# Differential attention on one core: the weighing of the last work tile ahead of the turning of the present one

## The reference, cut to what matters

```python
def _diff_attn(x, Wq, Wk, Wv, lq1, lq2, lk1, lk2, Wo, bo):
    q = (x @ Wq.T).reshape(b, n, H, D, 2).transpose(0, 1, 4, 2, 3).reshape(b, n, 2 * H, D) * scale
    k = (x @ Wk.T).reshape(b, n, H, D, 2).transpose(0, 1, 4, 2, 3).reshape(b, n, 2 * H, D)
    v = (x @ Wv.T).reshape(b, n, H, 2 * D).transpose(0, 2, 1, 3)
    att = softmax(nan_to_num(einsum('bnqd,bnkd->bnqk', q, k)))
    att6 = att.reshape(b, n, 2, H, 2, H)
    att2 = att6[:, :, 0, :, 0, :] - lam * att6[:, :, 1, :, 1, :]
    out = einsum('bnah,bhnd->bnad', att2, v)
    out = _rmsnorm(out) * (1.0 - LAMBDA_INIT)
    return out.reshape(b, n, d) @ Wo.T + bo
```

## Time and profile before

| what | us |
|---|---|
| median of 3 executions | 3107.2 (3105.85 to 3109.8) |
| the profiled execution, its own time | 3109.19 |
| its span in the profile | 3107.4 |
| differential attention, from the first scores to the last weighing | 2635.6 to 2728.3 |

### The profile page before, as it was taken

The page is one execution under the profiler, slowest core; times in us unless marked ns, Lnnn a source line. Parts: engine busy times, 40 slices in busy tenths (PEclk is TensorE's granted clock), DMA queues, the critical chain, the costliest instruction groups (busy, mean ns, idle before and its releaser), DMA issues. The chain is left out here.

```text
span 3107.4 us, 55478 instructions
## 1 busy us (share of the span) xinstructions
PE 2913.5 (94%) x23641; PEld 2312.9 (74%) x23644; DVE 1612.5 (52%) x3377; ACT 1191.8 (38%) x1885; POOL 84.0 (3%) x67
## 2 busy tenths in 40 slices
PE   6998997999989999999999999999999978689987
PEld 3444776788877888888888888888888867567864
DVE  4333523544454555555554555555555464764487
ACT  2212222333233444344433444334443331635675
POOL 0000101000000000000000000000000013010000
PEclk9999998999999999999999999999999989689988
DMA  7987010111211111101110111101111017705300
GB/s 262 319 288 255 1 44 25 41 41 61 81 51 49 46 47 33 32 28 47 46 33 25 36 47 46 33 23 38 46 41 41 29 45 149 77 31 166 115 15 28
DMA packets 174040, 222.36 MB, mean 72 GB/s; under 512 B 56416, under 2 KB 109664, under 8 KB 173424
## 3 DMA queue, kind: packets, MB, share of 16 engines
q1 hardware_dynamic: 146064, 198.01, 21.1%
q10 hardware_dynamic: 27744, 20.98, 3.0%
HBM read 206.36 MB, written 10.49 MB: 70 GB/s over the span
## 5 line engine op out<-in xcount | busy, mean ns | idle before, releaser
L91 PE MATMUL xa_J<-xa_c_hi,xa_wk_hi 128*128 128x402 f32 x1024 | 364.5, 356 | 4.3 <-ACT xa_kT L1944 3.0
L2056 DVE CUSTOM_DVE_ANT_0 xa_pr<-xa_S,xa_m 128x402 f32<-128x402 f32 x512 | 271.0, 572 | 166.0 <-PE xa_S L2205 166.0
L92 PE MATMUL xa_J<-xa_c_lo,xa_wk_hi 128*128 128x402 f32 x1024 | 354.1, 346 | 0.0
L93 PE MATMUL xa_J<-xa_c_hi,xa_wk_lo 128*128 128x402 f32 x1024 | 354.1, 346 | 0.0
L91 PE MATMUL xa_J<-xa_wv_hi,xa_c_hi 128*128 128x512 f32 (+1 forms) x832 | 335.3, 403 | 0.0
L93 PE MATMUL xa_J<-xa_wv_hi,xa_c_lo 128*128 128x512 f32 (+1 forms) x832 | 327.3, 393 | 0.0
L92 PE MATMUL xa_J<-xa_wv_lo,xa_c_hi 128*128 128x512 f32 (+1 forms) x832 | 327.3, 393 | 0.0
L1944 ACT ACTIVATE xa_kT<-xa_J,cl_bk 128x402 f32<-128x402 f32 x256 | 151.7, 593 | 457.5 <-PE xa_J L93 457.5
L2083 DVE TENSOR_TENSOR cl_v<-xa_J,cl_bv 128x512 f32<-128x512 f32 (+1 forms) x208 | 143.5, 690 | 262.0 <-PE xa_J L93 224.3
L1960 ACT ACTIVATE xa_pr<-xa_pr,xa_nm 128x1608 f32<-128x1608 f32 x128 | 208.6, 1632 | 95.0 <-DVE xa_nm L2072 95.0
L91 PEld LDWEIGHTS xa_J<-xa_c_hi,xa_wk_hi 128*128 128x128 f32 x1024 | 192.7, 188 | 66.3 <-ACT xa_kT L1944 42.9
(11 more groups left out here) (461 smaller groups left out, 5499.1 us busy)
## 6 DMA issues: line engine op xcount, KB each, us to landing
bl_rows<-in_ctx SPq DMA_DIRECT2D x40, 1024.0 KB, 8.3
main_x<-in_ctx_cols SPq DMA_DIRECT2D x192, 201.0 KB, 3.0
bl_cols<-in_ctx_cols SPq DMA_DIRECT2D x24, 1024.0 KB, 10.4
main_qoT<-in_L_ffn_w ACTq DMA_DIRECT2D x32, 512.0 KB, 3.8
main_x<-in_ctx_cols SPq DMA_DIRECT2D x64, 197.5 KB, 2.7
moe_raw<-in_L_ffn_routed_w SPq DMA_DIRECT2D x24, 512.0 KB, 4.1
main_qoT<-in_L_attn_W SPq DMA_DIRECT2D x16, 512.0 KB, 3.7
bl_early<-in_ctx SPq DMA_DIRECT2D x8, 768.0 KB, 12.6
```

Of the source, the lines that this page charges most:

```text
L91: pe.matmul(out, w_hi, x_hi, start=first, stop=False)
L92: pe.matmul(out, w_hi, x_lo, start=False, stop=False)
L93: return pe.matmul(out, w_lo, x_hi, start=False, stop=last)
L2056: nc.vector.tensor_tensor_reduce(out=pr[:, r, ks], in0=S[:, r, 0:KG], in1=m[:, ks], scale=1.0, scalar=NEVER, op0=ALU.add, op1=ALU.max, acc ...
```

## The change

In TensorE's loop over the work tiles the call of `weigh(w - 1)` moves from the end of the round to a place ahead of `turn(w)`. Nothing else changes.

```diff
                 for w in range(WORK):
                     if w + 2 < WORK:
                         scores(w + 2)
+                    if w:
+                        weigh(w - 1)
                     turn(w)
                     if w >= 2:
                         if w - 2 == QUARTERS:
                             pe.wait_ge(ms_ready, 1)
                         mean_squares(w - 2)
-                    if w:
-                        weigh(w - 1)
                 turn_spread(0)
```

## The result

| kernel | median us | runs | ratio to the kernel before, 95% interval |
|---|---|---|---|
| before | 3108.5 | 6 | 1 |
| changed | 3119.5 | 6 | 1.0034 [1.0023, 1.0045] |

0.34% of 3108.5 is 10.6 us, between 7.1 and 14.0. The forecast was +5.8 us (3113.0), in a range to 3121. So the sign and the range held and the size was too small: 3119.5 lies above the forecast's own band (3110 to 3117) and in the band of rival C (3119 to 3123). The profiled execution of the changed kernel took 3116.28 us, the fastest of its six, against 3109.19 for the one of before.

What follows compares the result with a forecast made beforehand. No engine fills the stretch; waits set it, and after the change a serial TensorE-ScalarE loop. Turn(1) +1.7, turn(2) +3.0, five rounds +4.3, tail -3.2 give +5.8 us: 3113.0 us, range for 8 in 10 3103 to 3121.

Steps and rivals of the forecast that it cites:

- the forecast's own band: Whole kernel: the likeliest case, +2.5 to +10 us, its own range 3110 to 3117 us; chance 0.6.
- rival C: Rounds all at half clock, 10.9 us, and one more stand: +12 to +16 us, 3119 to 3123; chance 0.12.
- The serial loop: TensorE with ScalarE, per tile: turn, widen, keep, weigh, next turn, nothing overlapping; 10.0 us a round.
- turn(1), later than before by: TensorE: turn(1) starts at 2661.0 behind weigh(0), against 2659.28 before; +1.7 us.
- turn(2), later than before by: TensorE: turn(2) starts at 2675.9 behind weigh(1), against 2671.22 before; +3.0 us more, to 4.7.
- five rounds, turn(2) to turn(7): TensorE's loop: five rounds of 10.0 us for the 45.7 there were; +4.3 us.
- tail, turn(7) to the end of weigh(7): End of the stage: 8.1 us where it was 11.33, as weigh(6) moved ahead of turn(7); -3.2 us.
- The expected gain: VectorE's three stops for scores: weigh leaves TensorE's path, 5.6 us instead of 9.2; up to 9.64 us back.
- The stand in weigh(1): TensorE waits for program at weigh(1)'s 73rd multiplication, 3.8 us, moving turn(2) from 2672.0 to 2675.9.
- rival A: No wait for program in weigh(1): turn(2) at 2672.0, +1.9 us, 3109; chance 0.18.
- Rival B: Loop at full clock price of 8.4 us, no stand, VectorE the bound: 6.2 us earlier, 3101; chance 0.1.

Runs made afterwards that it cites:

- e1: Changed kernel with keep(w-1) ahead of widen_all(w) on ScalarE; 3111.6 us, ratio 1.0009 to the kernel before.
- e7: The changed kernel run again, nothing edited; 3118.9 us, ratio 1.0034 to the kernel before.
- e2: Changed kernel with extra identity transposes, result unused, ahead of weighings 1 to 6; 3114.5 us, ratio 1.0022 to the kernel before.
- e12: Changed kernel with 20 small unused products (40 multiplications in the trace) ahead of turn(0); 3119.0 us, ratio 1.0034 to the kernel before.
- e9: Changed kernel with keep ahead of the four copies and unused identity transposes ahead of the weighings; 3109.6 us, ratio 1.0000 to the kernel before.
- e4: Kernel before with ScalarE's exp(w+1) moved behind widen_all(w); 3122.8 us, ratio 1.0047 to the kernel before.
- e3: Changed kernel with ScalarE's exp(w+1) moved between widen_all(w) and keep(w-1); 3125.3 us, ratio 1.0051 to the kernel before.

## Why the prediction was right in kind and low in size

**The serial loop** was right: turn, copies, keep, weigh, next turn, every turning after turn(0) and every weighing of tiles 1 to 6 was released as forecast. e1 takes one link out and gives its size back.

**Its price was the term that was mis-sized.** The prediction put "1.64 + 5.24 + 3.03 + 0.1 = 10.0 us a round", and by a second way 1.09 and 3.6. The first took the mean pieces of the kernel before, the second a turning at full clock with a weighing at half. In the profile the weighings 2 to 6 all take 3.64 us and the turnings 2 to 6 1.97, 1.97, 1.72, 1.48 and 1.36, 1.70 in the mean: 1.70 + 5.24 + 3.64 + 0.1 = 10.7. Measured is 53.5 us for the five rounds (2676.26 to 2729.75), 55.1 in e7, against 50.0.

| term | forecast | profile after | e7 |
|---|---|---|---|
| turn(1), later than before by | 1.7 | 1.3 | 0.0 |
| turn(2), later than before by | 4.7 | 3.2 | 3.6 |
| five rounds, turn(2) to turn(7) | 50.0 | 53.5 | 55.1 |
| tail, turn(7) to the end of weigh(7) | 8.1 | 7.5 | 7.7 |
| stage against before | +5.8 | +7.2 | +9.4 |

The error is in the clock: the weighings were all at their slow length, and none of the turnings 2 to 6 was at the 1.09 of full clock. In e7 a later gap of 1.82 us in weigh(4) comes on top, which the sum had at nothing; the gap of 1.14 us in scores(7) stood ahead of a wait for `squared` and cost nothing. The round's error of 3.5 us is partly hidden in the total, by luck: turn(2) came 1.5 us sooner than forecast and the tail was 0.6 us shorter. e2 shows the clock's part: with the idle time ahead of the weighings filled, four of six are fast and some 3.7 us come back.

**The expected gain went** nowhere useful. Scores do stand nearer to the turning (5.6 us of work instead of 9.2), but the turning itself comes later, so VectorE still waited 4.34, 1.25 and 2.37 us for scores (8.0 in all, 9.6 before), and 4.17 more for the mean squares that TensorE had to make behind a late turning.

**The stand in weigh(1)** came at its place, 3.3 us in length against 3.8. Its price was wrong: rival A took it away and expected 3109, e12 took it away and turn(3) came no sooner, for the keys' DMA is behind it. That wait was not in the prediction at all. By the Trainium skill, "Runtime: NRT & Kernel Launch", section "Instruction fetch mechanics", crossing a block is mostly hidden; in this stage every profile has gaps of 1 to 6 us at some of the edges.

**Rival B** (full clock, VectorE the bound) did not happen, and e9 shows what it would have needed. **Rival C** (half clock throughout, one more stand) is half true: its round of 10.9 us was nearer than the forecast's 10.0, while its slow tail did not come. The measured +10.6 lies between it and the forecast's own upper end. **The tail** was right to 0.6 us.

The median's 10.6 us (7.1 to 14.0) and the stages of the two profiles, +7.2 and +9.4, do not contradict each other; where inside that interval the true size lies stays open.

That the edges are transfers of program is inferred, from their spacing, from e12's shift and from the "instruction" queue. Its packets can be read one by one in the trace. Taking the time at which a packet is logged as its start, in the changed kernel the packets at 2643.0, 2661.8 and 2670.4 took 2.4 us each, and the three stands ended 1.5 to 1.9 us after the end of one (at 2646.88, 2666.11 and 2674.61); in e12 the one at 2696.2 took 1.6 us, and the stand in weigh(3) ended 1.4 us after its end. No run changed that transfer alone. Whether the serial loop would cost anything if keys and values were there from the start was not tried.

## What to carry to other kernels

Before putting a consumer ahead of the next producer on one engine, write down the ring of waits through the other engines and add up one turn of it; where each link waits for the last, its sum is the round, whatever the busy shares are. Where TensorE is left idle inside that ring, price the piece that follows at its low clock; here that was 3.64 us for a weighing in place of 1.99. When an instruction moves on an engine, ask for each of its results who waits: in e4 the move of one exp closed a second ring of 10.4 us a round; and before counting a removed stall as a gain, look for the transfer that stands right behind it.

## What the runs showed of the hardware that was not expected

- TensorE can stand still for 1 to 6 us at places 127 multiplications (with their weight loads 254 instructions) apart. 40 multiplications put in front moved the pattern by 40 and left the total as it was.
- 96 added transposes made the changed kernel a little faster (1.0022 against 1.0034, intervals that overlap). A weighing of 128 multiplications took 1.99 us in e2 behind work or 1.5 to 1.7 us of idle time, and 3.64 us in the changed kernel behind 2.0 to 4.6 us of it.
- The second half's keys came 42.8 to 45.0 us after the first scores in seven runs, however early TensorE was ready for them, so a stand ahead of that wait cost nothing.
- exp moved behind the square root on ScalarE brought a table load of 1.28 us with it (e3, e4).
